# First layer norm of the first sequence: one pass per tile, or a statistics pass and an apply pass

## What is computed

```python
x = x + attention(layernorm(x))     # x: (16, 2048, 1024), 16 heads of 64
x = x + ffn(layernorm(x))           # 1024 -> 4096 -> 1024
def layernorm(x, eps=1e-5):
    m = jnp.mean(x, axis=-1, keepdims=True)
    v = jnp.var(x, axis=-1, keepdims=True)
    return (x - m) / jnp.sqrt(v + eps)
```

## Time and profile before

| | us |
|---|---|
| runs of the kernel before | 3981.97 and 4066.08, median 4024.03 |
| the profiled execution | 3980.59 |
| its span on the slowest core (1) | 3978.8 |
| spans of all cores | 3950.1 to 3978.8 |
| busy in the span: TensorE, ScalarE, VectorE, GpSimd | 2651.2, 2367.8, 2079.1, 670.0 |

### The profile page before, as it was taken

One profiled execution on the slowest core, in us unless ns is written; L12 is line 12 of the kernel. 1 busy time (PEld: TensorE's weight loads), 2 busy tenths in 40 slices (PEclk: granted clock), 3 DMA queues, 4 the chain that ended last, 5 costly groups with the idle time before them and its releaser, 6 DMA issues.

```text
span 3978.8 us, 41405 instructions; the slowest of 8 cores (3950.1 to 3978.8 us)
## 1 busy us (share of the span) xinstructions
PE 2651.2 (67%) x10880; PEld 933.9 (23%) x10880; DVE 2079.1 (52%) x3166; ACT 2367.8 (60%) x2861; POOL 670.0 (17%) x1234
## 2 busy tenths in 40 slices
PE   0494767677686987766857344666667666757676
PEld 0241211111112421211211111222222222223232
DVE  2203443434341134343434258787877777777894
ACT  1231848667581267675848157676767676666772
POOL 1010000000001100000000224333333333333440
PEclk9997988888898998898989667788888787878898
DMA  5122111010103200101010564343444443444451
GB/s 107 51 37 90 30 47 38 14 44 4 45 4 75 32 3 4 44 4 45 4 44 4 109 93 66 63 83 55 80 69 72 72 75 61 83 67 73 66 81 50
DMA packets 204577, 207.53 MB, mean 52 GB/s; under 512 B 23744, under 2 KB 167104, under 8 KB 204352
## 3 DMA queue, kind: packets, MB, share of 16 engines
q0 software_dynamic: 169792, 95.82, 19.1%
q1 hardware_dynamic: 34560, 109.07, 8.5%
HBM read 257.52 MB, written 33.55 MB: 73 GB/s over the span
## 4 chain that ended last, share of the span: by engine, by line
PE 29%; DVE 17%; DVEq 17%; ACT 16%; issue 9%; DMA 7%; ACTq 4%; POOL 1%; SPq 0%; POOLq 0%
ACT PTb L625 12%; PE pAT L639 6%; PE pA L329 6%; DMA xstream<-x 5%; PE pA L612 5%; DVEq L962 5%; DVEq L1016 4%; DVE ft L985 4%; DVE fki L1017 4%; PE pBT L641 4%; DVEq L984 3%; PE pA L1070 3%; PE pA L363 3%; ACTq L1003 2%; DVEq L1098 1%
## 5 line engine op out<-in xcount | busy, mean ns | idle before, releaser
L625 ACT ACTIVATE PTb<-pA,negB 128x1024 bf16<-128x1024 f32 x1024 | 1108.3, 1113 | 475.1 <-PE pA L615 451.9
L935 PE MATMUL pA<-xn,w1s 128*128 128x512 bf16 x2048 | 622.3, 464 | 470.6 <-ACT ft L949 450.2
L798 POOL DMA_DIRECT2D w1s<-w x1024 | 559.3, 583 | 1057.1 <-PE pA L935 1030.9
L639 PE MATMUL pAT<-PTb,vtm 128*65 128x512 bf16 x1024 | 411.5, 402 | 269.7 <-ACT PTb L625 202.9
L1070 PE MATMUL pA<-w2b,gbuf 128*128 128x512 bf16 x2048 | 473.9, 392 | 97.3 <-ACT gbuf L1038 97.3
L612 PE MATMUL pA<-qfm,kfm 64*128 64x512 bf16 x1024 | 407.3, 408 | 49.8 <-DVEq L713 48.5
L935 PEld LDWEIGHTS pA<-xn,w1s 128*128 128x128 bf16 x2048 | 219.0, 112 | 847.2 <-issue 706.6
L641 PE MATMUL pBT<-PTb,vtm 128*65 128x512 bf16 x1024 | 411.3, 402 | 0.0
L615 PE MATMUL pA<-qfm,kfm 64*128 64x512 bf16 x1024 | 407.4, 408 | 0.0
L582 POOL DMA_DIRECT2D attn<-stgB x64 | 33.5, 523 | 1740.6 <-PE pBT L641 1274.5
L1070 PEld LDWEIGHTS pA<-w2b,gbuf 128*128 128x128 bf16 x2048 | 205.9, 101 | 358.9 <-issue 137.3
(11 more groups left out here) (90 smaller groups left out, 3222.3 us busy)
## 6 DMA issues: line engine op xcount, KB each, us to landing
w1s<-w POOLq DMA_DIRECT2D x1024, 64.0 KB, 2.7
xstream<-x SPq DMA_DIRECT2D x80, 512.0 KB, 4.0
x1rd<-x1s SPq DMA_DIRECT2D x64, 512.0 KB, 4.1
x1s<-x1t SPq DMA_DIRECT2D x32, 512.0 KB, 3.0
out<-outt SPq DMA_DIRECT2D x64, 256.0 KB, 2.3
wstr<-wqkv POOLq DMA_DIRECT2D x96, 128.0 KB, 5.1
w2b<-w POOLq DMA_DIRECT2D x32, 256.0 KB, 26.0
attn<-stgB POOLq DMA_DIRECT2D x64, 64.0 KB, 1.9
```

The source lines that it names most:

```text
L625: sc.activation(PT[:, kt % 2, :], pA[:, off:off + 1024], AF.Exp, bias=negB[:, 0:1], scale=SCALE).then_inc(c_s.sem, 1)
L639: t.matmul(pAT[0:65, :], lhs[:, 2 * pr, :], PT[:, kt % 2, 0:512], start=(kt == 0), stop=(kt == NKT - 1), skip_group_check=True)
L798: gp.dma_start(out=w1s[:, sl, dc, :], in_=w1[dc * 128:(dc + 1) * 128, grp * 256:(grp + 1) * 256]).then_inc(c_lw[sl].sem, 16)
L935: ins = t.matmul(pA[:, hb * 512:(hb + 1) * 512], w1s[:, sl, dc, (hm % 2) * 128:(hm % 2 + 1) * 128], xn2[:, bi % 2, dc, :], start=(dc == 0) ...
```

## The change

Three helpers replace both ways of doing the layer norm ahead of attention: `ln1c_stats` (load, statistics into `lnS`), `ln1c_finish` (epsilon, one Sqrt, reciprocal, product for 16 tiles) and `ln1c_tile` (load again, apply, transposes, copy). They are the code of sequence 1 with the sequence as an argument. Sequence 0 now runs 16 x `ln1c_stats`, `ln1c_finish`, 16 x `ln1c_tile` ahead of its q products; sequence 1 is done as before. Three waits are new: the apply waits for the transposes of the tile two before it (the last readers of its half of `xntm`), the first statistics of a pass wait for the last apply that read `lnS`, and the q, k and v products of sequence 0 wait for the copies of the tiles they read instead of for all tiles at once.

```diff
+        def ln1c_stats(sq, tt):
+            par = tt % 2
...
+                sy.dma_start(out=xstream[:, par, :],
+                             in_=x[sq, tt * 128:(tt + 1) * 128, :]
+                             ).then_inc(s_x[par].sem, 16)
...
+                v.wait_ge(s_x[par].sem, w)
+                if ag is not None:
+                    v.wait_ge(c_s.sem, ag)
+                v.bn_stats(ln2d[:, par, 0:6], xstream[:, par, 0:512])
+                v.bn_stats(ln2d[:, par, 6:12], xstream[:, par, 512:1024])
+                v.drain()
+                v.bn_aggr(lnS[:, tt, 0:2], ln2d[:, par, 0:12])
...
+            c_v.n += 1
+            xg[par] = ("v", c_v.n)
...
+        def ln1c_tile(sq, pi, ready):
...
+            def ev(sc, pi=pi, par=par, w=ldv, rg=(ready if pi == 0 else None),
+                   tg=ln1_tr_prev.get(par)):
+                sc.wait_ge(s_x[par].sem, w)
+                if rg is not None:
+                    sc.wait_ge(c_v.sem, rg)
+                if tg is not None:
+                    sc.wait_ge(c_pe.sem, tg)
+                sc.drain()
+                sc.activation(xntm[:, par, :], xstream[:, par, :], AF.Identity,
+                              bias=lnS[:, pi, 2:3],
+                              scale=lnS[:, pi, 1:2]).then_inc(c_s.sem, 1)
...
-                for i in range(NTT + 2):
-                    if i < NTT:
-                        ln_L(i)
-                        ln_V1(i)
-                        ln_S(i)
-                    if 0 <= i - 2 < NTT:
-                        ln_EV(i - 2)
-                    if 0 <= i - 1 < NTT:
-                        ln_V2(i - 1)
-                        ln_T(i - 1)
+                for tt in range(NTT):
+                    ln1c_stats(0, tt)
+                rdy = ln1c_finish(first=True)
+                for tt in range(NTT):
+                    xn_ev[tt] = ln1c_tile(0, tt, rdy)
...
-                               xw=xn_done, wl=wload[(s, g_)], pafv=pa_free_v):
+                               xw=(xn_ev[4 * tb + 3] if (s == 0 and mq == 0) else
+                                   (xn_done if gi == 0 else None)),
+                               wl=wload[(s, g_)], pafv=pa_free_v):
```

More of the change, by code:

```diff
@@ L179, in build, with ev @@
         ln1b_prev_ev = [None]
+        ln1_lnS_guard = [None]
+        ln1_tr_prev = {}
+        xn_ev = {}
+        def ln1c_stats(sq, tt):
+            par = tt % 2
+            def ev(sy, sq=sq, tt=tt, par=par, g=xg.get(par)):
+                if g is not None:
+                    sy.wait_ge(c_s.sem if g[0] == "s" else c_v.sem, g[1])
+                sy.dma_start(out=xstream[:, par, :],
+                             in_=x[sq, tt * 128:(tt + 1) * 128, :]
+                             ).then_inc(s_x[par].sem, 16)
+            p.on("sync", ev)
+            s_x[par].n += 16
+            ldv = s_x[par].n
+            def ev(v, tt=tt, par=par, w=ldv,
+                   ag=(ln1_lnS_guard[0] if tt == 0 else None)):
+                v.wait_ge(s_x[par].sem, w)
[5 more added lines that the diff above has]
+                v.bn_aggr(lnS[:, tt, 0:2], ln2d[:, par, 0:12])
+                v.drain()
+                v.engine_nop().then_inc(c_v.sem, 1)
+            p.on("vector", ev)
+            c_v.n += 1
+            xg[par] = ("v", c_v.n)
@@ new lines, in ln1c_finish, with ev @@
+        def ln1c_finish(first=False):
+            def ev(v, w=c_v.n):
+                v.wait_ge(c_v.sem, w)
+                v.tensor_scalar(lnS[:, :, 2:3], lnS[:, :, 1:2], 1e-5, None, ALU.add)
+                v.drain()
+                v.engine_nop().then_inc(c_v.sem, 1)
+            p.on("vector", ev)
+            c_v.n += 1
+            def ev(sc, w=c_v.n, first=first):
+                sc.wait_ge(c_v.sem, w)
+                if first:
+                    sc.wait_ge(c_lc.sem, ldw_consts)
+                sc.drain()
+                sc.activation(lnS[:, :, 3:4], lnS[:, :, 2:3],
+                              AF.Sqrt).then_inc(c_s.sem, 1)
+            p.on("scalar", ev)
+            c_s.n += 1
+            def ev(v, w=c_s.n):
+                v.wait_ge(c_s.sem, w)
+                v.reciprocal(lnS[:, :, 1:2], lnS[:, :, 3:4])
+                v.drain()
+                v.scalar_tensor_tensor(lnS[:, :, 2:3], lnS[:, :, 0:1], -1.0,
+                                       lnS[:, :, 1:2], ALU.mult, ALU.mult)
+                v.drain()
+                v.engine_nop().then_inc(c_v.sem, 1)
+            p.on("vector", ev)
+            c_v.n += 1
+            return c_v.n
@@ L354, in ev @@
                     def ev(t, s=s, g_=g_, nb=nb, tt=tt, bi=bi, pg=psg.get(gi - 4),
-                           vo=v_vones, wl=wload[(s, g_)]):
+                           vo=v_vones, wl=wload[(s, g_)],
+                           xw=(xn_ev[tt] if s == 0 else None)):
                         if pg is not None:
                             t.wait_ge(c_s.sem if pg[0] == "s" else c_v.sem, pg[1])
+                        if xw is not None:
+                            t.wait_ge(c_v.sem, xw)
                         if tt == 0:
@@ L387, in build @@
                 for tt in range(NTT):
[L388 to L396, removed]
@@ L490, in build @@
+                    ln1c_stats(1, tt)
+                ln1b_ready = ln1c_finish()
+                def ln1b_tile(pi):
+                    xn1s1[0] = ln1c_tile(1, pi, ln1b_ready)
             pending2 = [None]
```

121 lines of the change are left out of this document (38 added, 83 removed).

## The result

The changed kernel took 3944.03 us in the median of 11 runs (3937.93 to 4055.67), the kernel before 4062.79 us in 10 runs beside it. Their ratio is 0.9891, 95% interval [0.9848, 0.9934]. A second measurement of the same kernel, on another job (experiment e10), gave 0.9921 [0.9876, 0.9966].

A forecast was written before the change was run, and what follows sets the result against it. Sequence 0's normalisation was taken as latency-bound, one load in flight. Tile 15's statistics at 80.3, plus 3.26 + 1.28, 15 x 2.7 and 2.6, put the first product at 127.9, not 162.57: 3980.6 - 34.7 = 3945.9 us, range 3918 to 3995.

The forecast's parts named there:

- one tile per 8.2 us until 49 us: First pass of sequence 0 while weights land: tiles 2, 3 and 4 come 8.2 us apart, tile 4 at 49.4.
- the step from the time to the size of the change: Whole kernel: 3946 us from the 3980.6 us profiled execution, 0.9% less; the median of before was 4024.03.
- The sum's stations: Sequence 0: tile 15's statistics 80.3, first apply 84.8, apply 15 at 125.3, first product 127.9; 34.7 us earlier.
- the sign "about 8 us apart": First pass: sign of being right, first statistics of tiles 2 to 4 about 8 us apart, then 2.8.
- The table load: Between sequence 0's passes: Sqrt's table load on ScalarE, uncovered there, adds 1.28 us before the first apply.
- The second pass: Sequence 0's applies: 2.7 us a tile, bounded by 2.15 (pT buffer) below and 3.6 (landing time) above.
- The edits at nothing: New waits of apply and v products, and unchanged queue order of sequence 2's loads, cost nothing; weights land by about 50.
- my 94% for "within 2%": Whole kernel: 94% chance that the change stays within 2%, about 80 us; 4% faster, 2% slower than that.
- (a): Rival, both passes: loads go one at a time, first product at 157, gain 5, 3975 us; chance 4%.
- (b): Rival: mild contention, and the pT chain (transposes, copy and release) sets the second pass; 3922 us; chance 12%.
- (c): Rival, behind the first stage: lower granted TensorE clock, 28.7 us per 0.010, 4003 us at 0.020 less; chance 5%.
- (d): Rival: products overlap no normalisation, already counted so; overlap would give up to 15 us more; no chance given.

The follow-up runs named there:

- e10: The changed kernel unedited, measured again beside the kernel before on another job's chip; ratio 0.9921 [0.9876, 0.9966].
- e1: Changed kernel, but in both passes of sequence 0 a load of x waits for the tile just before it; 4095.08 and 4104.71 us.
- e2: Kernel before, single pass, with four buffers for x instead of two in sequence 0's layer norm; ratio 0.9886 [0.9779, 0.9993].
- e4: Changed kernel with four buffers for x instead of two in both passes of sequence 0; ratio 0.9885 [0.9794, 0.9976].
- e3: Changed kernel, but sequence 0's first pass leaves all 16 x tiles in SBUF and its second issues no loads; ratio 0.9895 [0.9863, 0.9927].
- e9: As e8, with each block's eviction on ScalarE put one tile later, behind the next apply; ratio 0.9716 [0.9673, 0.9758] to the kernel before.
- e7: Changed kernel with four x buffers, projection weights' loads and VectorE's bias-constant operations moved behind sequence 0's layer norm; quickest runs 3899.95 and 3901.86 us.
- e8: Against the kernel before: single pass, four x buffers, late constants and weights, first q group's blocks placed behind tiles' transposes; ratio 0.9758 [0.9644, 0.9871].

## Where the prediction was right, and where it was wrong

**The two steps that failed.** One is a term of the sum: one tile per 8.2 us until 49 us, because a second load in flight was to win no part of the busy DMA engines. It won one: a tile took 5.3 us. The sum came out only because the steps behind were longer than taken, which is luck. The other is the step from the time to the size of the change: 3946 was worked out from one undisturbed execution (3980.6) and put beside a median of 4024, as a gain of 78 us within a noise of 80, where 43 us (ratio 0.9891), 31 (0.9921) and 35.8 (median spans) were measured, all clear of no change. The mechanism, a loop held up by one load at a time and a first pass that has two, was right.

**The time.** 3945.9 us was worked out, 3944.03 is the median. The sum's stations: tile 15's statistics 80.3, measured 80.85; first apply 84.8, 85.45; last apply 125.3, 126.03; first product 127.9, 128.33; gain 34.7, 34.2 (33.8 and, in e10, 35.1 on the mean of cores). That the stations lie within 1 us is in part chance: two errors cancelled (below), and the cores of one profile alone differ by 4 to 7 us in the first product.

**What bounds the kernel.** Shown from both sides: with one load in flight two passes are slower than before (e1); with four the old single pass loses nearly all its waits for DMA, 4.2 us of 80.4 being left (e2).

**The term of the sum that was wrong: one tile per 8.2 us until 49.** Measured 5.3 (two tiles from 33.28 to 43.84): from 25.16 on, tiles came at 33.28, 37.45, 43.84, 48.08, so tiles 2 to 5 and not 2 to 4 were through by 49, and the sign "about 8 us apart" didn't come for tiles 3 and 4. Tile 4 was 5.6 us ahead of the 49.4 in the sum. The sharing then lasted longer (tile 6 at 54.10, 6.0 us after tile 5), and from there to tile 15 the mean step was (80.85 - 54.10) / 9 = 2.97 and not 2.81. The misses cancelled to half a microsecond. The case for 8.2 leaned on rows with one load in flight, and 8.2 is the mean of their two waits (8.98 and 7.42) without the 1.7 us of statistics that come on top. Under the same weights x moved at a tile per 10.5 us with one in flight (e1), 5.3 with two (changed kernel), 3.6 with four (e4, 36.72 to 44.03). Beside it stood the rule of the Trainium skill (DMA: Bandwidth & Descriptors, Queues, rings and completion order) that an engine goes round between queue rows packet by packet, from which I drew that a second load in the same queue adds no part. The runs don't bear out that inference. They don't show the rings themselves, so the rule may still hold there; why more transfers in one queue draw a larger part stays open.

**The table load** of 1.28 us did fall between the passes, at 83.07. **The second pass:** 40.58 / 15 = 2.71 us a tile, taken 2.7. Its floor is 2.05 (e3, e4), I had 2.15. Its loads are the limit, as taken: without them it is 8 to 11 us shorter (e3).

**The edits at nothing.** No run took the new waits out, so their cost by themselves wasn't tried; the sum leaves them under 1 us. Weights were no limit: the first product began 0.8 us after the start of the last transposes.

**The size against the noise.** "About 2% is what a measurement of this kernel can tell from no change" was too coarse: the two intervals, [0.9848, 0.9934] and [0.9876, 0.9966], both exclude no change, so the kernel is faster by about 1%, and my 94% for "within 2%" says less than the data do. And 3946 set against the median of 4024 reads as 1.9% less, about twice the 1.1 and 0.8% that were measured; set against the profiled execution on which the sum was made, it is 0.9%. Only the second comparison means anything, and I should have given the ratio as the forecast.

**The rivals.** (a) one load at a time: excluded, and e1 shows what it would have cost, 198 and not 157, because statistics and landing then add up. (b) mild contention and the pT chain: half of it happened, see the term above. (c) a lower granted clock behind: not seen; the granted clocks are 0.854 to 0.859 in e10's profile, 0.854 to 0.864 before. Its price of 28.7 us per 0.010 was read from two cores 0.010 apart, within what cores differ by anyway; the two lines of the profiled execution above give 59.7 us for 0.028, or 21 per 0.010. (d) no overlap with products: so, by TensorE's order; e9 is 35 us quicker than the nearest run without overlap (e7), more than the 15 us I named for an overlap, though the single pass has its part in that.

## What to carry to other kernels

When a loop waits for DMA while every engine idles, count the loads in flight first: two buffers give two in flight only if nothing in the loop waits for the landed load ahead of the instruction that frees the other buffer. Depth (more buffers, borrowed from tensors not yet written) gave more here than loading everything twice. When work is laid into a neighbour stage's gaps, put its evictions behind the work that the loop itself waits for.

## What was not expected of the hardware

The part of busy DMA engines that one queue draws grew with its transfers in flight. SP's queue on core 4 from 28 to 48 us, while weights land, in e1 (one load in flight), the changed kernel (two) and e4 (four):

```profile
q1 hardware_dynamic: 342, 1.26, 20.9%
...
q1 hardware_dynamic: 574, 2.10, 35.0%
...
q1 hardware_dynamic: 764, 2.81, 46.2%
```

GpSimd's queue had 88.7, 72.0 and 58.2% beside it, for 2.43, 1.92 and 1.56 MB. So a MB of weights, as the trace counts it, took about 7.4 us of all engines and a MB of x 3.3, in all three: at the same share of 1.07 the GB/s rise when more of the traffic is x, and say nothing of the engines' limit by themselves.

From 30 to 70 us, with a tile's transposes and a block of products in turn, TensorE on core 2 was granted a mean clock of 0.61 in e8, where it stood idle for 2.3 us ahead of most transposes, and 0.83 in e9, where some of these gaps are gone (cores 1 and 4: 0.79 and 0.70 against 0.91 and 0.96). The mean matmul of that stretch fell from 26.46 us / 102 to 28.28 / 150, 0.26 to 0.19 us. So an order that keeps TensorE fed also made its work cheaper, which the expectation of e9, with all blocks at 1.2 GHz, had left out.
